# Residual, norm statistics and power two sequences at a time in the first three seams of a two-layer perceiver, with fewer spare products

## The reference

```python
x = x + _L0_xattn_ref(ctx_1024, ctx_1024, _layernorm(x, axis=-1), mask_BxS2_if0, ...)
x = x + _L0_attn_ref(_layernorm(x, axis=-1), ...)
x = x + _L0_ffn_ref(_layernorm(x, axis=-1), ...)
x = x + _L1_xattn_ref(_layernorm(x, axis=-1), ctx_1024, ctx_1024, ...)
x = x + _L1_attn_ref(_layernorm(x, axis=-1), ...)
x = x + _L1_ffn_ref(_layernorm(x, axis=-1), ...)
...
def _layernorm(x, axis=-1, eps=1e-05):
    m = jnp.mean(x, axis=axis, keepdims=True)
    v = jnp.var(x, axis=axis, keepdims=True)
    return (x - m) / jnp.sqrt(v + eps)
```

## Time and profile before

| | us |
|---|---|
| median of 3 runs | 285.39 |
| the three runs | 280.69, 286.51, 285.39 |
| the profiled execution | 280.6 |
| its span, first to last instruction | 278.8 |
| PE busy, share of the span | 89% |
| DVE busy | 65% |
| ACT busy | 46% |
| POOL busy | 22% |

### The profile page before, as it was taken

How to read it: one execution, slowest core, us unless ns; L and a number is a source line. 1 busy time by engine, 2 the same in 40 slices (tenths; PEclk the granted TensorE clock), 3 DMA queues, 4 the chain that set the end, 5 groups by cost and what they waited for, 6 DMA issues and landing times.

```text
span 278.8 us, 5215 instructions
## 1 busy us (share of the span) xinstructions
PE 249.0 (89%) x2042; PEld 185.7 (67%) x2042; DVE 181.3 (65%) x492; ACT 128.3 (46%) x270; POOL 60.5 (22%) x80
## 2 busy tenths in 40 slices
PE   8986977988898988899998998868897999999995
PEld 8644755766564674244494665347785999999995
DVE  6884878776557666999855667777689755424111
ACT  1158868741552206233303965874234554363331
POOL 5069910000200019476401001030341010100000
PEclk9999999997999999999999999997999999999999
DMA  7952000002990220000000000000000000000000
GB/s 201 348 198 116 2 5 0 2 2 43 411 432 21 56 98 0 0 2 1 0 0 5 2 2 0 0 2 0 4 0 0 2 1 0 2 0 21 0 0 22
DMA packets 5678, 13.98 MB, mean 50 GB/s; under 512 B 2193, under 2 KB 3729, under 8 KB 5010
## 3 DMA queue, kind: packets, MB, share of 16 engines
q1 hardware_dynamic: 4208, 10.73, 10.5%
q10 hardware_dynamic: 1442, 2.87, 3.1%
HBM read 13.34 MB, written 0.26 MB: 49 GB/s over the span
## 4 chain that ended last, share of the span: by engine, by line
PE 59%; DVE 19%; POOL 8%; ACT 6%; issue 4%; DMA 2%; SPq 1%; DVEq 0%; ACTq 0%
PE BK L2344 10%; PE BK L2329 9%; PE BK L2108 7%; PE BK L2212 3%; PE BK L2185 3%; PE BK L1811 3%; PE BK L2196 2%; PE BK L1941 2%; PE BK L2302 2%; PE BK L2136 2%; DVE WTF L1366 2%; PE BK L2058 2%; DMA boff_sb<-boff_dram 2%; ACT WTF L864 2%; PE BK L2038 1%
## 5 line engine op out<-in xcount | busy, mean ns | idle before, releaser
L2329 PE MATMUL BK<-XT,WTF 128*128 128x256 f32 x128 | 30.5, 381 | 1.1 <-ACT WTF L949 1.1
L2344 PEld LDWEIGHTS BK<-WTF 128*128 128x128 f32 x256 | 30.9, 192 | 0.8
L2344 PE MATMUL BK<-WTF 128*128 128x128 f32 x256 | 31.0, 275 | 0.0
L949 ACT ACTIVATE WTF<-BK 128x512 f32<-128x512 f32 x32 | 18.8, 596 | 23.9 <-PE BK L2329 23.8
L2108 PE MATMUL BK<-XT,WTF 128*128 128x512 f32 x64 | 29.2, 596 | 0.3 <-DVE WTF L1417 0.2
L1811 PE MATMUL BK<-ident 128*128 128x128 f32 x210 | 27.3, 284 | 0.0
L1811 PEld LDWEIGHTS BK<-ident 128*128 128x128 f32 x210 | 25.8, 198 | 2.2 <-issue 2.2
L791 ACT ACTIVATE WTF<-BK 128x512 f32<-128x512 f32 x40 | 22.5, 597 | 7.7 <-PE BK L1903 7.1
L1706 DVE SCALAR_TENSOR_TENSOR X<-BK,CW,X 128x128 f32<-128x128 f32 x32 | 9.7, 346 | 24.7 <-PE BK L2344 24.7
L2329 PEld LDWEIGHTS BK<-XT,WTF 128*128 128x128 f32 x128 | 23.1, 190 | 4.0 <-ACT WTF L949 1.5
L613 POOL TENSOR_TENSOR RSTD<-VE,MHALF 128x2 f32<-128x2 f32 x8 | 5.5, 707 | 77.9 <-DVE VE L1038 77.9
(11 more groups left out here) (297 smaller groups left out, 465.7 us busy)
## 6 DMA issues: line engine op xcount, KB each, us to landing
WTF<-w_f_dram SPq DMA_DIRECT2D x2, 2048.0 KB, 14.5
WTF<-w_c_dram SPq DMA_DIRECT2D x1, 2048.0 KB, 7.8
decay<-c_decay_dram ACTq DMA_DIRECT2D x1, 1024.0 KB, 6.2
decay<-mask_q_dram SPq DMA_DIRECT2D x1, 1024.0 KB, 6.3
crows_sb<-c_rows_dram ACTq DMA_DIRECT2D x1, 544.0 KB, 5.9
w_e_sb<-w_e_dram SPq DMA_DIRECT2D x1, 480.0 KB, 4.2
w_b_sb<-w_b_dram SPq DMA_DIRECT2D x1, 384.0 KB, 5.5
WTF<-win_dram SPq DMA_DIRECT2D x1, 320.0 KB, 4.9
```

The costliest lines, as they stand in the source:

```text
L949: act.activation(GT[:, e % 2, 2 * p:2 * p + 2, lane_cols(h)], lane_bank(h, 2 + p).rearrange("p (a n) -> p a n", a=2), ACT.Gelu).then_inc(e ...
L2329: ins = pe.matmul(lane_bank(h, 2 + p)[:, 256 * i:256 * i + 256], w_f1[:, o:o + P], XT[:, lane_cols(h)], start=True, stop=True)
L2344: ins = pe.matmul(lane_bank(h, e % 2)[:, i * P:(i + 1) * P], GT[:, e % 2, j, b * P:(b + 1) * P], w, start=(j == 0), stop=(j == 3))
```

## The change

`residual` takes over the statistics: for each half it adds, waits for that addition, takes `bn_stats` of two sequences, `bn_aggr` of two, and writes VE, and then starts on the other half. `stats` is no longer called in stages B, C and D. In stage C the identity's copy and the mask are written ahead of the residual. On TensorE the three groups of 3 spare products at the end of stage A become one group of one, the 5 ahead of B's norm go, the 13 ahead of C's become 6 and the 13 ahead of D's become 7. No arithmetic of the result is changed. The lines of the changed kernel stand up to 8 further down than those of before.

```diff
--- before.py
+++ after.py
@@ -1066,12 +1066,20 @@
                                   T0[:, 0:2, :].rearrange("p r (h d) -> p r h d", h=H), AX.X, ALU.add).then_inc(l_mix, 1)
                 dve.wait_ge(l_mix, 1)
 
-            def residual(s, other, at=halves_of(7, 5)):
+            def residual(s, n, other, at=halves_of(7, 5)):
 
                 for h in range(2):
                     pair = slice(2 * h, 2 * h + 2)
                     dve.wait_ge(proj_ps, 2 * PROJ.index(s) + 1 + h)
                     dve.tensor_tensor(X[:, pair, :], at[h], other[:, pair, :], ALU.add).then_inc(x_ready, 1)
+                    stage_done(dve, PROJ.index(s) + 1, h)
+                    for b in (2 * h, 2 * h + 1):
+                        ins = dve.bn_stats(STAT[:, b, :], X[:, b, :])
+                    settle(ins)
+                    for b in (2 * h, 2 * h + 1):
+                        ins = dve.bn_aggr(MV[:, b, :], STAT[:, b, :])
+                    settle(ins)
+                    dve.tensor_scalar(VE[:, pair], MV[:, pair, 1], EPS, None, ALU.add).then_inc(ln_var, 1)
 
             def over(ap, n, axis=1):
 
@@ -1340,9 +1348,8 @@
                         ins.then_inc(ga_ctx, 1)
                         dve.wait_ge(ga_once_ps, 4)
                         dve.tensor_copy(CT[:, :, :], by_b(bank(4))).then_inc(ga_ctx, 1)
-                    residual("A", X)
+                    residual("A", LN_B, X)
                 if s == "B":
-                    stats(LN_B, X, of_stage(s))
                     tail_values()
                     norm(LN_B, X, XH)
                     dve.wait_ge(loads["w_b"], 16)
@@ -1370,9 +1377,8 @@
                     dve.wait_ge(b_oT, B)
                     dve.wait_ge(b_wide_ps, 1)
                     dve.tensor_tensor(CTT[:, :].rearrange("p (b t) -> p b t", b=B), T1[:, :, :], BK[:, 0:4, 0:P], ALU.mult)                       .then_inc(b_on, 1)
-                    residual("B", X, halves_of(7, 6))
+                    residual("B", LN_C, X, halves_of(7, 6))
                 if s == "C":
-                    stats(LN_C, X, of_stage(s))
                     norm(LN_C, X, XH)
                     dve.wait_ge(r_lg_ps, 1)
                     lg = BK[:, 4, 0:B * NE].rearrange("p (b e) -> p b e", b=B)
@@ -1434,12 +1440,11 @@
                         share(e, 1)
                         if 2 <= e < 6:
                             tail(e - 2)
-                    dve.wait_ge(xb_ready, 1)
-                    residual("C", XH, down_halves)
-                if s == "D":
                     dve.tensor_copy(identh[:, :], ident[:, :])
                     dve.tensor_scalar(MB[:, :], mtail[:, :], 0, MASKED, ALU.is_equal, ALU.mult).then_inc(d_mb, 1)
-                    stats(LN_D, X, of_stage(s))
+                    dve.wait_ge(xb_ready, 1)
+                    residual("C", LN_D, XH, down_halves)
+                if s == "D":
                     tail_flag()
                     norm(LN_D, X, XH)
                     dve.memset(GALL, 0.0)
@@ -2015,13 +2020,10 @@
                     pe.wait_ge(a_vs, UNITS)
                     pe.wait_ge(a_z, 4)
                     add_row(halves_of(7, 5)[1], bias_row[:, ROWS["bo"]], 2)
-                    stay_warm(2, 3)
                     pe.wait_ge(ctxT_ready, 1)
                     project_half(wo, 0, 7)
-                    pe.wait_ge(a_soft, 15)
-                    stay_warm(2, 3)
                     pe.wait_ge(a_mix, 4)
-                    stay_warm(2, 3)
+                    stay_warm(2, 1)
                     turned(1)
                     pe.wait_ge(ctxT_ready, 2)
                     project_half(wo, 1, 5)
@@ -2031,7 +2033,6 @@
                     pe.wait_ge(proj_ps, 2)
                     pe.matmul(BK[:, 4, 0:D], w_b[:, 4 * D:5 * D], centre, start=True, stop=True).then_inc(b_v_ps, 1)
                     tail()
-                    stay_warm(2, 5)
                     norm_T(LN_B, 7)
                     pe.wait_ge(ln_xT, xT_count(LN_B))
                     for j in range(4):
@@ -2090,7 +2091,7 @@
                     project_half(wo_gn[:, :], 0, 7)
                     project_half(wo_gn[:, :], 1, 6)
                 if s == "C":
-                    stay_warm(3)
+                    stay_warm(3, 6)
                     norm_T(LN_C, 7)
                     pe.wait_ge(ln_xT, xT_count(LN_C))
                     pe.wait_ge(loads["w_c"], 48)
@@ -2159,7 +2160,7 @@
                     pe.wait_ge(flag_rows, 2)
                     pe.wait_ge(e_g, 2 * NE)
                     pe.matmul(BK[:, 0, 0:1], ones[:, :], FLD[:, :], start=True, stop=True).then_inc(flag_sum, 1)
-                    stay_warm(1)
+                    stay_warm(1, 7)
                     norm_T(LN_D, 7)
                     pe.wait_ge(ln_xT, xT_count(LN_D))
                     pe.matmul(bank(6), w_d[:, 2 * D:3 * D], XT[:, :], start=True, stop=True).then_inc(d_q_ps, 1)
```

## The result

| | before | changed |
|---|---|---|
| median of 20 executions, us | 285.06 | 287.23 |
| lowest to highest | 278.59 to 291.77 | 283.55 to 293.37 |
| ratio to before, with its 95% interval | | 1.0185 (1.0124 to 1.0245) |
| the profiled execution: span, mean granted clock | 278.8, 0.988 | 286.9, 0.935 |

The change makes the kernel slower by 1 to 2%. The ratio compares only executions that lie near the fastest of their kernel; the medians differ by 0.8%, the means (284.8 and 287.7) by 1.0%.

What follows compares the result with a forecast made beforehand. Bound: the chain through VectorE, GpSimd, TensorE and ScalarE at three seams, mostly TensorE between. Terms of -2.25 and clock +3.3 gave +1.05 on 280.6, or 281.65; halfway to 286.4 gave 284.0 us, range 278.3 to 288.5.

Steps and rivals of the forecast that it cites:

- the level: Whole kernel: median halfway between 281.65 on the profiled execution's level and 286.4 on the median's, so 284.0 us.
- My sum: Whole kernel: four terms of -2.25 us and clock terms of +3.3 make +1.05 us on the profiled 280.6.
- A's end: -1.8: End of stage A: fewer spare products let the turning start 2.0 us earlier, less 0.2 for the lower clock.
- the 0 of the seam from A to B: Stage A to B: splitting the statistics gains nothing, because `tail`'s products cover them; 0 us (-0.1 to +0.2).
- My second rival: From A's end through B's projections: the clock, once down, stays down; +4.6 us, 287.6 in the middle, chance 0.15.
- C's start: +1.4: Start of stage C: with six spare products the clock falls and slows the large products; +1.4 us (0 to +3.0).
- the cover of 0.2 us: Start of stage C: the turning of the router's weights waited only 0.23 us for VectorE, hiding 0.2 of a slowdown.
- B's start: +1.6: Start of stage B: without five spare products the clock falls over the four projections; +1.6 us (0 to +3.2).
- the seam from B to C: Stage B to C: both halves arrive together, so the split pays nothing; +0.1 us (-0.2 to +0.3).
- the seam from C to D: Stage C to D: halves arrive apart, so the second power ends earlier; -0.55 us (-0.7 to -0.2).
- D's seven products: Start of stage D: seven spare products instead of thirteen leave a short gap; clock term +0.3 us (0 to +1.6).

Runs made afterwards that it cites:

- stage A filled: The changed kernel with spare products also added inside stage A; mean 286.5 us, ratio 1.0056 to the kernel before.
- thin spares only: The kernel before, VectorE's order unchanged, with only the reduced spare products of the change; mean 289.5 us, ratio 1.0246.

## Why the prediction was wrong

The forecast was 284.0, a little under the median of before, most likely no change that can be told; measured is 287.2, a loss that its interval clears. The sum was too low by one term, and the level then turned its sign.

**The step that failed first is the level.** My sum was +1.05 us, a loss. I then set the changed kernel halfway between its sum on the profiled execution and on the median, which turned the loss into a number below the median shown. That supposed that what tells the executions apart is independent of the change. It is the clock: 0.31 to 0.34 us per us at the lower clock tells most of the executions' times, and the change adds to that time (23 us to 34 on average, at least 24), so no changed execution reaches the level of the profiled one before (7 us at the lower clock). The trace of before had a full clock at C's start and one low stretch at A's end; that was one draw of several, not the kernel.

**A's end: -1.8 was mis-sized, and the 0 of the seam from A to B with it.** "I take 0.2, since the clock of before came back about here with a busier TensorE": it did not come back. The turning came 2.0 earlier against its sums as worked out, but projection and `tail` ran at the lower clock: -1.2 up to the second residual, +1.1 from there to B's projection, so 8.82 became 8.74: -0.1. That was no accident of one execution: all six traces with the thin end and nothing added there have 2.47 or 2.48 for the first part and 6.24 to 7.26 for the second. My second rival described this and had 0.15; in one trace (stage A filled) it ran right through B's projections. With the clock held the two parts are -1.95 (6.86 or 6.87 in three traces).

**C's start: +1.4 was right in size, though the fall was not new there.** With six spare products the part to the turning of the router's weights took 9.52, 7.85, 9.52, 9.51 and 9.46 in five traces (mean 9.2), with 13 it took 6.54, 9.52, 7.85, 6.54, 7.83 and 7.83 in six (mean 7.7), with 13 and 2 behind the turnings 6.53 or 6.54 three times. So the clock fell there with 13 as well, in four of six, and the 6.54 of the trace of before was a good draw; against it alone the price looks like +2.6. Up to the residual at the end of C the means are 39.95 and 38.61: +1.3. What TensorE loses there beyond the cover of 0.2 us, the turning of the router's weights loses.

**B's start: +1.6 was right in size.** The profile after showed nothing of it, and that was its luck: the projections alone lost 1.5 to 2.4 in the four other traces without the five products. From B's first projection to the residual at its end the five took 24.57, 27.68, 27.68, 26.27 and 26.97, mean 26.6; with the five products, and nothing added behind the turnings, it was 24.56 or 24.57 six times: +2.1, of which a part is a second low stretch later in B (in two of the five traces).

Added up from these averages, A's end (8.97 against 8.89) is +0.1, B +2.1, C +1.3 and the two seams -0.4: +3.1, beside 2.9 +- 1.0 between the mean times before and after. The forecast had +0.75 for the same places, and 1.9 of the gap is A's end. Each average is of a few single executions and good to about 0.6.

**Right in size:** the seam from B to C (+0.1, measured +0.11), the seam from C to D (-0.55, measured -0.54), the statistics in the seam from A to B covered by `tail`. The gain of the split is the -0.4 of the two together. **Not settled:** D's seven products. The clock fell right behind D's first projection in one of six traces with seven (thin spares only, down from 154 to 158 us) and in none of eight with thirteen; the other low stretches come at least 38 us later. The stretch from D's projection to the end varied between 128.9 and 131.6 with seven and between 128.9 and 130.4 with thirteen.

## What to carry to other kernels

Products whose result nobody reads can still set the time: price the removal of spare products by the clock of what runs behind them, the product right behind the gap and the ones after it, and put those that must stay where TensorE waits anyway (ahead of a branch, behind a turning while another engine copies) and not ahead of the instruction on the path. When executions of one kernel differ by more than the change is worth, find what tells them apart before choosing a level; here the mean granted clock of each execution did it. A forecast should not be anchored on the profiled execution when it is the best of the draws, and a price read from one profile after is a draw too: here it showed B's start as free and C's as twice its average.

## What the runs showed that I had not expected

The clock fell while the page called TensorE busy. In the changed kernel TensorE was busy 3.41 of 4 us from 12 to 16 us (columns as above), and then the clock was down to 33 us:

```profile
12.00:16.00 4.00, 3.41 (x17) 1.57 (x14) 3.76 (x11) 1.19 (x2) 0.00 (x0) 1.00 0.76 234
16.00:20.00 4.00, 4.00 (x11) 2.19 (x10) 3.79 (x8) 1.57 (x3) 3.30 (x5) 0.53 0.88 292
```

The same code before, a little denser, kept it:

```profile
12.00:16.00 4.00, 4.00 (x23) 1.94 (x19) 3.79 (x10) 0.73 (x2) 0.00 (x0) 1.00 0.64 216
16.00:20.00 4.00, 4.00 (x20) 2.23 (x18) 3.79 (x8) 2.11 (x4) 3.37 (x5) 1.00 0.67 207
```

But the kernel before also kept it through a stretch in which TensorE was busy half the time, and beyond:

```profile
36.00:40.00 4.00, 1.95 (x29) 1.63 (x21) 3.48 (x9) 2.54 (x6) 0.00 (x0) 1.00 0.01 2
40.00:44.00 4.00, 3.75 (x62) 2.84 (x62) 2.61 (x9) 3.28 (x7) 0.00 (x0) 1.00 0.03 6
```

So the busy share of the stretch ahead did not tell here whether the clock would hold. What did was not found: products of a bias row, one row deep, take some 1.6 us from 12 to 16 us in both traces, the one that kept the clock and the one that lost it. The Trainium skill, page "TensorE: Matmul & The Clock Gate", section "What's actually happening", says that the cold products at a kernel's start vary from run to run and puts that ramp under 1% of a typical span. No trace here shows that ramp: the row from 0 to 4 us has a granted clock of 1.00 in the profiles before and after. For the falls in the middle of this kernel the variation agrees and the size does not: 7 to 44 us at the lower clock in the kernel before, 278.3 to 292.6 us in time.
